# Attention stack on one core: two lanes of side work in phase 2, rounding of the context moved among the maxima, new paddings in the written order, and query projections of 112 columns

## What is computed

```python
q = (h @ wq).reshape(b, n, heads, dh).transpose(0, 2, 1, 3)      # h: (layer norm of) x, 56 rows
k = (ctx @ wk).reshape(b, m, heads, dh).transpose(0, 2, 1, 3)    # 1500 keys (1496 in block 3)
v = (ctx @ wv).reshape(b, m, heads, dh).transpose(0, 2, 1, 3)
attn = jax.nn.softmax(jnp.einsum('bhnd,bhmd->bhnm', q, k) * scale)
out = jnp.einsum('bhnm,bhmd->bhnd', attn, v) ... @ wo + bo
# heads 20, 8, 20; dh 64, 20, 8
```

## Time and profile before

| | |
|---|---|
| time before, median of 3 runs | 6340.44 us (6320.77 to 6346.13) |
| profiled execution | 6339.04 us, its span 6337.3 us |
| busy: PE, PEld | 5771.7, 4691.9 us |
| busy: DVE, ACT, POOL | 2831.6, 3120.8, 3093.7 us |
| mean granted TensorE clock | 0.953 |
| DMA queue of the data | 108.56 MB, 6.0% of 16 engines |

### The profile page before, as it was taken

How to read it: one execution, slowest core, us unless ns; L and a number is a source line. 1 busy time by engine, 2 the same in 40 slices (tenths; PEclk the granted TensorE clock), 3 DMA queues, 4 the chain that set the end, 5 groups by cost and what they waited for, 6 DMA issues and landing times.

```text
span 6337.3 us, 92395 instructions
## 1 busy us (share of the span) xinstructions
PE 5771.7 (91%) x34384; PEld 4691.9 (74%) x34384; DVE 2831.6 (45%) x4978; ACT 3120.8 (49%) x7280; POOL 3093.7 (49%) x3472
## 2 busy tenths in 40 slices
PE   7999999999999999988888888899999999999998
PEld 5777777777777777766666666677777777777776
DVE  2444444444444444424555554344444554444452
ACT  1454555545444455544444444255555555555554
POOL 0344444444444444444454455155555555555555
PEclk8899999999999999988999999599999999999998
DMA  2000000000000000000010111000000000000000
GB/s 53 12 15 15 15 15 15 12 15 15 15 15 15 15 15 13 10 19 21 27 28 24 27 28 36 6 18 15 18 15 16 18 21 15 15 15 17 15 19 10
DMA packets 84427, 114.47 MB, mean 18 GB/s; under 512 B 42814, under 2 KB 64682, under 8 KB 83978
## 3 DMA queue, kind: packets, MB, share of 16 engines
q1 hardware_dynamic: 83978, 108.56, 6.0%
HBM read 104.06 MB, written 4.46 MB: 17 GB/s over the span
## 4 chain that ended last, share of the span: by engine, by line
PE 65%; DVE 12%; issue 8%; POOL 7%; ACT 5%; DMA 4%; POOLq 0%; SPq 0%; ACTq 0%; DVEq 0%
PE ps_c L683 13%; PE ps_c L1063 7%; POOL p_lo L1595 6%; PE ps_u L1136 6%; PE ps_s L1121 5%; PE ps_u L1138 5%; PE ps_u L1137 5%; PE ps_s L1123 4%; PE ps_s L1122 4%; PE ps_c L1082 3%; DVE mpiece L1439 2%; DVE uT L1466 2%; DMA w_area<-recs 2%; PE ps_c L889 1%; PE ps_c L863 1%
## 5 line engine op out<-in xcount | busy, mean ns | idle before, releaser
L1595 POOL TENSOR_TENSOR p_lo<-p,p_hi 125x448 fp32r<-125x448 f32 (+2 forms) x2688 | 2716.6, 1018 | 2655.2 <-ACT p_hi L1808 2593.6
L1806 ACT ACTIVATE p<-ps_s 125x448 f32<-125x448 f32 (+2 forms) x2688 | 1324.0, 493 | 2090.9 <-PE ps_s L1123 1973.2
L1439 DVE TENSOR_REDUCE mpiece<-ps_c 125x1 f32<-125x500 f32 (+1 forms) x1984 | 1249.7, 671 | 157.7 <-PE ps_c L1063 141.9
L1808 ACT ACTIVATE p_hi<-ps_s 125x448 fp32r<-125x448 f32 (+2 forms) x2688 | 1317.7, 490 | 0.0
L1136 PE MATMUL ps_u<-p_hi,ctx_hi 125*97 125x448 f32 (+2 forms) x2688 | 1005.0, 374 | 77.8 <-POOL p_lo L1595 71.6
L1121 PE MATMUL ps_s<-q_hi,ctxT_hi 105*125 105x448 f32 (+3 forms) x2688 | 988.7, 368 | 46.3 <-ACT p_hi L1808 26.6
L1063 PE MATMUL ps_c<-ctxT_hi,q_hi 96*125 96x500 f32 (+1 forms) x2112 | 856.2, 427 | 161.2 <-DVE mpiece L1439 71.6
L1122 PE MATMUL ps_s<-q_lo,ctxT_hi 96*125 96x448 f32 (+2 forms) x2688 | 931.2, 346 | 0.0
L1123 PE MATMUL ps_s<-q_hi,ctxT_lo 96*125 96x448 f32 (+2 forms) x2688 | 928.7, 346 | 0.0
L1138 PE MATMUL ps_u<-p_lo,ctx_hi 125*97 125x448 f32 (+2 forms) x2688 | 923.3, 343 | 0.0
L1137 PE MATMUL ps_u<-p_hi,ctx_lo 125*96 125x448 f32 (+2 forms) x2688 | 923.2, 343 | 0.0
(11 more groups left out here) (231 smaller groups left out, 5963.2 us busy)
## 6 DMA issues: line engine op xcount, KB each, us to landing
ctx_raw<-in_ctx SPq DMA_DIRECT2D x96, 562.5 KB
pT<-recs SPq DMA_DIRECT2D x32, 420.0 KB, 3.3
w_area<-recs SPq DMA_DIRECT2D x32, 420.0 KB, 3.3
w_area<-recs SPq DMA_DIRECT2D x32, 168.0 KB, 3.4
cs<-in_ctx SPq DMA_DIRECT2D x192, 6.0 KB, 2.9
x_between<-x_out SPq DMA_DIRECT2D x32, 80.0 KB
x_in<-x_between SPq DMA_DIRECT2D x32, 80.0 KB
w_area<-in_L_xattn_wq SPq DMA_DIRECT2D x2, 800.0 KB, 5.9
```

The costliest lines, as they stand in the source:

```text
L1439: z = V.tensor_reduce(mpiece[0:wide, k, r:r + 1], C(0, wide, n % banks(t), 0, PIECE), AX.X, ALU.max)
L1595: P.tensor_tensor(p_lo[0:kp, k % 3, 0:w], p32[0:kp, k % 2, 0:w], p_hi[0:kp, k % 3, 0:w].bitcast(F32), ALU.subtract).then_inc(*sig("pl_ready"))
L1806: A(p32[0:kp, k % 2, 0:w], ps_s[0:kp, k % 2, 0:w], ACT.Exp, scale=DH[t.ph] ** -0.5)
L1808: A(p_hi[0:kp, k % 3, 0:w], ps_s[0:kp, k % 2, 0:w], ACT.Exp, scale=DH[t.ph] ** -0.5)\
```

## The change

Four things, each in its own place:

- In the second half of a pair of phase 2, `context`, `queries` and `maxima` of the next pair form a lane of their own (slots 2 to 21) beside the rest of `pre` (slots 0 to 21). PE's `context` then no longer waits for `xm_ready`, but in the first pair.
- The rounding of the context into `ctx_hi` leaves DVE's `context` and stands in DVE's `maxima`, in three CASTs of four chunks each, ahead of maxima 2, 6 and 10 (1, 3 and 5 in phase 2: `HI_AT`). POOL's six subtractions follow each third. In phase 2 the first CAST waits until the products of the row before have read `ctx_hi`.
- Extras in `PARTS`: phase 1's `pre` at 8, 10, 14, 16, 18 and 30 larger, at 39 smaller; phase 3's at 9 and 15 larger, at 19 smaller; `queries` and `context` get one number more in phases 1 and 3 with an extra of 3, 2 and 6, 3.
- The query projection takes 2 x 56 = 112 moving columns instead of 128, and its PSUM places lie 112 apart.

```diff
+HI_AT = ((2, 6, 10), (1, 3, 5), (2, 6, 10))
...
-    "ctx_hi": ((2, 2, 2), 0), "ctx_lo": ((12, 12, 12), 1),
+    "ctx_hi": ((6, 6, 6), 0), "ctx_lo": ((12, 12, 12), 1),
...
-            "pre": ((40, 3, {4: 1, 7: 0.5, 8: 2, 14: 1, 16: 1.5, 18: 1.5, 22: 2, 27: 2, 34: 1, 35: 0.5, 37: 1, 38: 1.5,
-                             39: 4, 40: 4.5}), (29, 3.5, {5: 2, 15: 1.5, 22: 0.5, 23: 2}), (20, 2.5, {2: 3, 6: 1.5, 7: 0.5, 11: 0.5, 15: 0.5, 19: 4, 20: 1})),
-            "queries": ((6, 1, {}), (3, 3, {}), (6, 1, {})),
+            "pre": ((40, 3, {4: 1, 7: 0.5, 8: 3, 10: 1, 14: 1.5, 16: 3, 18: 2, 22: 2, 27: 2, 30: 1, 34: 1, 35: 0.5, 37: 1,
+                             38: 1.5, 39: 2, 40: 4.5}), (29, 3.5, {5: 2, 15: 1.5, 22: 0.5, 23: 2}), (20, 2.5, {2: 3, 6: 1.5, 7: 0.5, 9: 2, 11: 0.5, 15: 1, 19: 2, 20: 1})),
+            "queries": ((7, 1, {7: 3}), (3, 3, {}), (7, 1, {7: 2})),
...
-            "context": ((4, 1, {}), (4, 4, {}), (4, 1.5, {})),
+            "context": ((5, 1, {5: 6}), (4, 4, {}), (5, 1.5, {5: 3})),
...
-                head, norm = [pre], []
+                head, norm = [pre] if pre else [], []
...
-                parts, start, tail = [], 0.0, 0
-                if not last:
-                    parts, tail = before(t + 1, pre_b), TAIL
+                lanes = []
+                if not last and t.ph == 1:
+
+                    lanes = [lane(before(t + 1, ()), 2.0, TAIL), lane([pre_b], 0.0, TAIL)]
+                elif not last:
+                    lanes = [lane(before(t + 1, pre_b), 0.0, TAIL)]
...
-                            z = both(C(0, DC, g % banks(t), 128 * h, 128), lambda i: w_m[:, i, w:w + DC],
-                                     lambda i: hT[:, i, :, :])
+                            z = both(C(0, DC, g % banks(t), 2 * T * h, 2 * T), lambda i: w_m[:, i, w:w + DC],
+                                     lambda i: hT[:, i, :, 0:T])
...
-                                pe.wait_ge(*got("xm_ready", t, per("xm_ready", t)))
+                                if t.ph != 1 or t.it == 0:
+                                    pe.wait_ge(*got("xm_ready", t, per("xm_ready", t)))
...
-                    yield 1
-                    dve.wait_ge(*got("cr_loaded", t, 16 * (b + 1)))
-                    V.tensor_copy(ctx_hi[:, b, :, 0:DC], ctx_raw[:, :].rearrange("p (c d) -> p c d", c=NC))\
-                        .then_inc(*sig("ctx_hi"))
...
+                            if n in HI_AT[t.ph]:
+                                j = HI_AT[t.ph].index(n)
+                                if j == 0:
+                                    dve.wait_ge(*got("cr_loaded", t, 16 * (b + 1)))
+                                    if t.ph == 1 and b == 0 and t.it:
+
+                                        dve.wait_ge(*got("pv_done", t, -(per("pv_done", t) // 2)))
+                                V.tensor_copy(ctx_hi[:, b, 4 * j:4 * j + 4, 0:DC],
+                                              ctx_raw[:, 4 * DC * j:4 * DC * (j + 1)].rearrange("p (c d) -> p c d", c=4))\
+                                    .then_inc(*sig("ctx_hi"))
...
-                        yield 1 + (1 if t.ph == 1 else 2) * j
-                        if j == 0:
-                            pool.wait_ge(*got("ctx_hi", t, b + 1))
+                        yield 3 + HI_AT[t.ph][j // 2] + (j % 2) * (HI_AT[t.ph][1] - HI_AT[t.ph][0]) // 2
+                        if j % 2 == 0:
+                            pool.wait_ge(*got("ctx_hi", t, 3 * b + j // 2 + 1))
```

More of the change, by code:

```diff
@@ L520, in pair @@
                     weave(main(t, 0, first=first), lane(parts + end), *norm)
-                parts, start, tail = [], 0.0, 0
-                if not last:
-                    parts, tail = before(t + 1, pre_b), TAIL
+                lanes = []
[3 more added lines that the diff above has]
+                    lanes = [lane(before(t + 1, pre_b), 0.0, TAIL)]
                 elif t.ph < 2:
-                    parts, start = [part("pre", side.pre, At(t.ph + 1, 0, ahead=True))], POST + 4.0
-                weave(main(t, 1, last=last), lane(parts, start, tail), apart(side.normalise(t, 0)))
+                    lanes = [lane([part("pre", side.pre, At(t.ph + 1, 0, ahead=True))], POST + 4.0)]
+                weave(main(t, 1, last=last), *lanes, apart(side.normalise(t, 0)))
             for ph in range(3):
@@ L1397, in queries @@
                         V.tensor_tensor(q_lo[:, 0, q].rearrange("p (h s) -> p h s", h=4),
-                                        C(0, DC, g % banks(t), 0, 512).rearrange("p (h b s) -> p h b s", h=4, b=2)[:, :, 0, 0:T],
+                                        C(0, DC, g % banks(t), 0, 8 * T).rearrange("p (h b s) -> p h b s", h=4, b=2)[:, :, 0, :],
                                         q_hi[0:DC, 0, q].bitcast(F32).rearrange("p (h s) -> p h s", h=4),
@@ L1739, in queries @@
                         q = slice(4 * T * g, 4 * T * (g + 1))
-                        src = C(0, DC, g % banks(t), 0, 512).rearrange("p (h b s) -> p h b s", h=4, b=2)[:, :, :, 0:T]
+                        src = C(0, DC, g % banks(t), 0, 8 * T).rearrange("p (h b s) -> p h b s", h=4, b=2)
                         A(q_stage[:, q].rearrange("p (h s) -> p h s", h=4), src[:, :, 1, :], ACT.Copy)\
```

## The result

The changed kernel took **6162.28 us** (median of 4, 6148.83 to 6167.26), the kernel before beside it 6335.92 us: ratio **0.9729, interval 0.9709 to 0.9749**. So it is faster by 2.2 to 2.7%; the forecast was 6140 in a range of 6050 to 6275. The changed kernel repeats within 0.3%, the kernel before varies more. I compare the experiments with 6162 us.

A forecast was written before the change was run, and what follows sets the result against it. TensorE (PE), busy 5771.7 of 6337.3 us, was taken to set the time, with DVE late next in the maxima. Terms -41 - 66 - 38 + 38 - 67 - 25 = -199 took 6339 to 6140 us, range 6050 to 6275.

The forecast's parts named there:

- Queries, -41: Query projection: 3072 matmuls go from 128 to 112 columns, 13.3 ns saved each; -41 us, ends -41 and 0.
- Two lanes in phase 2, -67: Second halves of phase 2: a second lane fills waits, about 29 instead of 33.5 us; -67 us, ends -120 and +20.
- Room in phases 1 and 3, -66: Short attention's steps 8, 16, 30 (phase 1) and 9 (phase 3) written later, removing PE's waits; -66 us, ends -85 and -30.
- listed waits of PE, 84.8 us: PE's idle time on xn 26.5, sm 15.3, kvb 16.4 and p_hi 26.6 us, ahead of which the new room stands.
- Room ahead of the maxima, -38: Extras behind context and queries in phases 1 and 3 let PE work during its waits; -38 us, ends -77 and 0.
- the 77.0 us of waits: PE's waits ahead of the maxima, on ctxT_lo 42.5 and q_lo 34.5 us; half was counted as gain.
- Rounding among the maxima, +38: Three small CASTs on DVE cost 0.6 us for each of 64 stretches of phases 1 and 3; +38 us, ends 0 and +122.
- Clock, -25: Fewer stalls take a quarter of the low-clock 106 + 131 us out of phases 1 and 3; -25 us, ends 0 and -100.
- The sign that I gave: PEclk, PE's granted clock, above 0.98 in phases 1 and 3, where it was 0.98 and 0.97.
- DVE takes the place of the waits: Rival: room ahead of the maxima brings nothing and CASTs cost their whole 1.9 us a stretch; 6262 us, 17%.
- The slow rival: DVE-POOL lock: each of 288 CASTs waits a whole p_lo (1.15) and takes 0.3 us; +346 for +38, 6448 us, 5%.
- The lanes ran side by side: Opposite of a rival for phase 2's second halves: maxima wait for the chain, or uT meets ctx_lo; +67, 6207 us, 13%.

The follow-up runs named there:

- u_round2b1: Changed kernel with, for b = 1 of phase 2 alone, one rounding CAST ahead of the ctxT_lo subtractions and ctx_lo at its old place: 6171.3 us, ratio 0.9770.
- c_wide: Changed kernel without the room behind context, rounding on ACT, and phase 1 maxima at 2.5 in place of 2.25: 6157.3 us, ratio 0.9741 to the kernel before.

## Why the prediction was right, and where its steps were not

The total was right within 22 us, and that is in part luck. The two largest clean terms, queries and lanes, came out as forecast (107 of 108 us). The other terms on the written order (-66, -38 and +38) were to give 66 us together; the runs give -30, +48 and -15 for them, 3 us the wrong way, and the total still came out because the steps do more together than one by one (see below).

- **Queries, -41.** Right: 38 us when undone, 96.6 ns each. (The rows give 0.82 ns a column, not 0.83; nothing hangs on it.)
- **Two lanes in phase 2, -67.** Right: 69 us when undone, second halves at 28.9 for a forecast of 29.
- **Room in phases 1 and 3, -66.** Mis-sized: 30 us, and these largely by way of the clock. The step that failed is that listed waits of PE, 84.8 us, were taken as time ("Of 84.8 us I count **-66**"): they fell to 22.3, and halves at full clock kept their length in phase 1 and lost 0.8 us in phase 3. "Everything else in the lane is squeezed by 4 to 9%, which gives a little back" was what I priced too low. My test, first halves of phase 1 near 75, failed: 79.5.
- **Room ahead of the maxima, -38.** Wrong sign. The step that failed is "I let the 77.0 us of waits count half". I had seen that DVE is late next, and charged it only as a discount. The room behind `context` costs 69 us (rather 58, without phase 2), that behind `queries` brings 21: together +48. In the first halves of phase 1 it filled PE's wait while DVE's run of reductions started at the same 6.2 us.
- **Rounding among the maxima, +38.** Its place costs 51 us against leaving DVE free, so the price of the CASTs was right in kind (1.75 us a stretch for 1.9). Against its old place it gains 15 us as long as the other edits stand; that is not a clean price, since it is mixed with the clock. For b = 0 of phase 1 the old place is better, by 7 us or more.
- **Not foreseen: phase 2's first halves.** I had left them at nothing. They gained 1.7 us each. Before, the eight of 14 with a uT product of over 3.7 us lasted 35.0 to 40.0 us and the six without 30.5 to 32.1; in the changed kernel undisturbed ones take 31.3, and the five that lasted over 35 us had 10.2 or 13.7 us of low clock and no long product. I had the long product in the earlier trace rows, but only as a cost for the CASTs; the move of `ctx_lo` removed it. At their best these halves did not get shorter (30.5 before).
- **Clock, -25.** Low clock fell from 601 to 516 us, worth up to 42; 49 of these 85 us lie in the windows of phases 1 and 3 (255 to 206), worth up to 25, which is what I had written. The sign that I gave, a clock above 0.98 there, did not come: both stand at 0.98. It is not a term beside the others, as I wrote it, but the way in which some of them act (the room, the old place of the rounding).

The single steps undone, 69 + 38 + 30 - 48 + 15 = 104 us (113 with the 9 of u_round2b1), do not make up the 136 to 174 us between the kernels. Each step moves the clock too, and a step can be worth another amount without the others; which of these makes the rest is open.

The rival "DVE takes the place of the waits" (6262) had the mechanism of phase 1 and the wrong total: it is what happened in the first halves there (79.6 and 79.5 us), while phase 2 gave 101 us and phase 3 55. The slow rival, the lock with 1.45 us for each of 288 CASTs, did not come: mean 0.58 us. The lanes ran side by side.

## What to carry to other kernels

Before you give a step more room, look at what the engine that it waits for does next. If that engine has a closed run of work behind it (here DVE, 27 reductions and 15.00 of 15.00 us busy), the room fills PE's wait and moves nothing; take work off that engine instead (the rounding on ACT: 51 us, and 110 with the room removed). Room in a full lane is taken from its neighbours, and their waits grow; where a half is loose, as in phase 2, a second lane beside the first fills its waits (33.7 to 28.9 us for a half here).

## What the runs showed of the hardware

- The same work, with the same waits, ran a stretch of 17 us at 2.4 or at 1.2 GHz, in one execution (rows of c_wide). With it a kernel became 105 us slower where the two waits that grew most made 47, so small changes of the written order can't be read without the time at low clock beside them.
- A CAST of 125x384 took 341 ns at its least and 1280 at its most on DVE beside POOL, and 514 to 618 ns on ACT.
- A uT product of 96x448 with both inputs in SBUF took 0.6 to 1.6 us in the changed kernel. In phase 2 of the kernel before and of u_round2b1, 13 took 3.3 to 4.4 us; each ended 0.4 to 0.5 us behind the last of three or more POOL operations (`ctx_lo`, `p_lo`) that followed each other without a gap, so it spanned several of them and not one.
- A DVE reduction of 125x500 out of PSUM took 667 ns beside POOL's operations and 671 without.
